# A gated WKV and feed-forward layer on one core: the recurrence in another form, a fixed slot for every step, and weight parts requested by ScalarE

## What is computed

```python
k = layernorm(x)                          # over the channels
# WKV recurrence over the 1024 tokens, for each of the 1024 channels, v = ctx
no = max(o, u + k_t); A = exp(o - no); E = exp(u + k_t - no)
y_t = (A*p + E*v_t) / (A*q + E)
no2 = max(w + o, k_t); A2 = exp(w + o - no2); E2 = exp(k_t - no2)
p, q, o = A2*p + E2*v_t, A2*q + E2, no2
x = x + tanh(g_xattn) * y
X = float16(layernorm(x))
D = float16(gelu(X @ W0.T + bias0))       # W0 is [4096, 1024]
x = x + tanh(g_ffn) * float16(D @ W1.T + bias1)   # W1 is [1024, 4096]
```

## Time and profile before

| | |
|---|---|
| median of 3 runs (range) | 2145.67 us (2144.49 to 2146.55) |
| span of the profiled execution | 2146.2 us |
| busy: PE, DVE, POOL, ACT | 1888.6, 1103.5, 592.7, 586.7 us |
| mean granted TensorE clock | 0.939 |
| moved by DMA | 286.56 MB, mean 134 GB/s |

### The profile page before, as it was taken

One profiled execution on the slowest core, in us unless ns is written; L12 is line 12 of the kernel. 1 busy time (PEld: TensorE's weight loads), 2 busy tenths in 40 slices (PEclk: granted clock), 3 DMA queues, 4 the chain that ended last, 5 costly groups with the idle time before them and its releaser, 6 DMA issues.

```text
span 2146.2 us, 23175 instructions
## 1 busy us (share of the span) xinstructions
PE 1888.6 (88%) x8960; PEld 892.4 (42%) x8960; DVE 1103.5 (51%) x1250; ACT 586.7 (27%) x759; POOL 592.7 (28%) x394
## 2 busy tenths in 40 slices
PE   1046778978889997999999997999999999999999
PEld 1023334434434443444444443444444444444444
DVE  8979975998971148899311158899211000000000
ACT  3326553343433232443000133443000121110000
POOL 4636750455653122444000022444000000000000
PEclk6558889989989998999999998999999999999999
DMA  5424574535466434333333333333233322223331
GB/s 176 142 103 156 168 254 169 212 119 205 164 229 197 156 117 139 108 126 126 122 118 118 138 128 118 127 127 140 90 115 118 108 79 79 79 88 112 108 110 53
DMA packets 72285, 286.56 MB, mean 134 GB/s; under 512 B 7680, under 2 KB 7680, under 8 KB 65024
## 3 DMA queue, kind: packets, MB, share of 16 engines
q1 hardware_dynamic: 72192, 285.28, 37.8%
HBM read 218.14 MB, written 67.11 MB: 133 GB/s over the span
## 4 chain that ended last, share of the span: by engine, by line
PE 68%; DVE 17%; issue 8%; POOL 3%; DMA 2%; ACT 1%; SPq 0%; DVEq 0%; POOLq 0%; ACTq 0%
PE acc L921 36%; PE acc L893 29%; DVE uOE L734 3%; DVE uOE L731 2%; DVE uOE L703 2%; DVE uA L712 1%; PE trA L856 1%; PE trA L872 1%; DVE uR L717 1%; DVE uOE L727 1%; DVE uR L722 1%; DVE K L745 1%; DVE uOE L709 1%; DVE uR L741 1%; DMA xin<-x_in 1%
## 5 line engine op out<-in xcount | busy, mean ns | idle before, releaser
L893 PE MATMUL acc<-XT,W 128*128 128x512 f16 x4096 | 911.7, 385 | 60.4 <-ACT DT L533 52.5
L921 PE MATMUL acc<-DT,W 128*128 128x512 f16 x4096 | 900.1, 381 | 12.1 <-POOL W L411 12.1
L893 PEld LDWEIGHTS acc<-XT,W 128*128 128x128 f16 x4096 | 405.8, 99 | 554.5 <-issue 66.7
L921 PEld LDWEIGHTS acc<-DT,W 128*128 128x128 f16 x4096 | 401.5, 98 | 491.1 <-issue 23.4
L757 DVE SCALAR_TENSOR_TENSOR xo<-e,tg,xo 128x512 f32<-128x512 f16 x64 | 52.1, 814 | 626.8 <-ACT e L542 626.6
L533 ACT ACTIVATE DT<-acc,b 128x512 f16<-128x512 f32 (+1 forms) x256 | 173.1, 686 | 511.2 <-PE acc L893 510.9
L542 ACT ACTIVATE e<-acc,b 128x512 f16<-128x512 f32 x64 | 43.8, 684 | 676.8 <-PE acc L921 676.8
L378 POOL TENSOR_TENSOR rstd<-rstd,power 128x1 f32<-128x1 f32 x64 | 47.5, 742 | 611.8 <-DVE rstd L646 611.8
L741 DVE RECIPROCAL uR<-uR 128x512 f32<-128x512 f32 x64 | 209.6, 3314 | 0.0
L391 POOL TENSOR_TENSOR uOE<-uOE,uV 128x512 f32<-128x512 f32 x64 | 81.0, 1275 | 380.4 <-ACT uOE L502 233.7
L640 DVE BATCH_NORM_STATS2 stats<-trA 128x6 f32<-128x512 f32 x60 | 38.8, 689 | 218.8 <-PE trA L872 218.8
(11 more groups left out here) (54 smaller groups left out, 1000.2 us busy)
## 6 DMA issues: line engine op xcount, KB each, us to landing
W<-parts_dram SPq DMA_DIRECT2D x56, 2048.0 KB, 8.1
parts_dram<-W SPq DMA_DIRECT2D x64, 512.0 KB, 6.7
stage<-w_in SPq DMA_DIRECT2D x52, 512.0 KB, 6.0
uV<-vT_in SPq DMA_DIRECT2D x64, 256.0 KB, 2.7
xT<-xT_in SPq DMA_DIRECT2D x32, 512.0 KB, 5.2
x_dram<-K SPq DMA_DIRECT2D x32, 512.0 KB, 3.7
xo<-x_dram SPq DMA_DIRECT2D x32, 512.0 KB, 9.6
out<-xo SPq DMA_DIRECT2D x32, 512.0 KB, 7.9
```

The source lines that it names most:

```text
L893: mm = nc.tensor.matmul(acc[bank][:, :], W[:, slot, part, q, P * c:P * (c + 1)], XT[:, c, HALF * half:HALF * (half + 1)], start=(c == 0 an ...
L921: mm = nc.tensor.matmul(acc[bank][:, :], W[:, slot, part, q, P * c:P * (c + 1)], DT[:, nb, HALF * half:HALF * (half + 1)], start=(nb == 0 ...
```

## The change

It does six things.

1. **The recurrence loses its running maximum.** With decay = exp(min(w, 0)), kept in `decay`, it scans `q` and `p` directly with E = exp(k + shift); a positive part of w is taken care of by adding `grow` times the token's number to the normalised rows (one more VectorE pass for each tile of `x`, 128x1024). A unit is now seven VectorE operations of 512 elements (E times V, scan q, scan p, denominator, numerator, reciprocal, product), three tiny copies, one exponential on ScalarE and one sum on GpSimd (`residual`).
2. **`K` is gone.** TensorE transposes four blocks into a pair of PSUM banks (`unit_banks`), the exponential is made there in place, and VectorE works on E and E·V in PSUM. `copy_k` is gone with it. Four PSUM banks serve the front, one the float16 transposes, so three are left as accumulators (`BANKS = 3`).
3. **One unit at a time at a fixed slot.** A batch has 128 slots of 16 matmuls. `UNIT_SLOT`, `LN1_SLOT` and `LN2_SLOT` say at which slot each unit, tile of `x` and tile of the second norm stands; every engine walks the same slots. The program is unrolled.
4. **The parts are requested by ScalarE** (`load_parts` in its program), except the first of each new pass in batch 0; the constants too, ahead of everything on ScalarE.
5. **`xin` holds four tiles**, and they are loaded after the last unit that reads the four before.
6. **SyncE's order** follows the slots: in a unit's slot it loads V for n + 2, waits until unit n has been summed (`x2_done`) and loads xT for n + 4.

The diff, cut to its core:

```diff
+SLOTS = 4 * NB
-BANKS = 4
+BANKS = 3
+RING1, RING2 = 5, 3
+def place_front():
+    for i, k in enumerate((5, 6, 9, 12, 14, 17, 20, 22)):
+        UNIT_SLOT[CB + i] = k
+    for i, k in enumerate((37, 38, 41, 44, 46, 49, 52, 54, 64, 65, 68, 71, 73, 76, 79, 81)):
+        UNIT_SLOT[UNITS + i] = k
+    for i in range(HT):
+        LN1_SLOT[HT + i] = 1 + i
+        LN1_SLOT[2 * HT + i] = 33 + i
+        LN1_SLOT[3 * HT + i] = 60 + i
+        LN2_SLOT[HT + i] = (27 + i, 29 + i)
+    for i in range(TILES):
+        LN2_SLOT[TILES + i] = (88 + 2 * i, 90 + 2 * i)
...
+    for b in (1, 2):
+        at, n, T = SLOTS * b, UNITS * (b + 1), TILES * (b + 1)
+        for i, k in enumerate((1, 4, 8, 12, 16, 20, 24, 28, 37, 40, 44, 48, 52, 56, 60, 64)):
+            UNIT_SLOT[n + i] = at + k
...
+        for i in range(TILES):
+            LN2_SLOT[T + i] = (at + 72 + 6 * i, at + 75 + 6 * i)
...
+        def parts_to_w(engine, s):
+            engine.dma_start(W[:, s % 2, :, :, :].rearrange("p a q n -> p (a q n)"), parts_dram[s])\
+                .then_inc(w_landed[s % 2], 16)
...
+            def load_xT(n):
+                b, i = divmod(n, UNITS)
+                if n >= 4:
+                    sp.wait_ge(x2_done, n - 3)
...
+            def residual(n):
+                pool.wait_ge(y_done, n + 1)
+                pool.wait_ge(xT_landed[n % 4], 16 * (n // 4 + 1))
+                slot = X2[:, n % UNITS, :]
+                nc.gpsimd.tensor_tensor(slot, slot, S[:, n % 2, 1, 0:HALF], ALU.add).then_inc(x2_done, 1)
...
+            def exps(n):
+                act.wait_ge(kt_done, n + 1)
...
+                bank = unit_banks(n)[0]
+                nc.scalar.activation(bank, bank, ACT.Exp, bias=shift[:, n % CB:n % CB + 1]).then_inc(e_ready, 1)
...
+            def load_parts(s, groups):
+                act.wait_ge(mm_done, groups)
+                parts_to_w(act, s)
...
+                    if b == 0 and NB <= k < 2 * NB - Q and k % Q == 0:
+                        load_parts((k - NB) // Q + 1, k)
+                    if b and k % (2 * Q) == 0 and not (b == B - 1 and k == SLOTS - 2 * Q):
+                        load_parts((k // (2 * Q) + 1) % (2 * STEPS),
+                                   GROUPS * b if k == 0 else group_of(b, k - 1) + 1)
+                    for n in UNITS_AT.get(K, ()):
+                        exps(n)
+                    if K in X2_AT:
+                        copy_xt(X2_AT[K])
+                    if k < GROUPS1:
+                        gelu(b, k)
+                    elif k % Q == Q - 1:
+                        round_e(b, (k - GROUPS1) // Q)
+                    if b == 0 and k < NB - 2 * Q:
+                        hi_piece(k + 2 * Q)
...
+            def norm_x(T):
+                row = xin[:, T % HT, :]
+                dve.wait_ge(rstd_done[0], T + 1)
+                nc.vector.tensor_scalar(row, row, mv[:, 0, T % 2, 0:1], rstd[:, 0, T % 2, 1:2],
+                                        ALU.subtract, ALU.mult).then_inc(xn_done, 1)
...
+                nc.vector.scalar_tensor_tensor(row, grow[:, :], negt[:, T % TILES:T % TILES + 1], row,
+                                               ALU.mult, ALU.add).then_inc(xn_ready, 1)
...
+            def unit(n):
...
+                nc.vector.tensor_copy(S[:, j, :, 0], state[:, i, :]).then_inc(seeded, 1)
+                dve.wait_ge(e_ready, n + 1)
+                nc.vector.tensor_tensor(EV, E, V[:, j, :], ALU.mult).then_inc(ev_done, 1)
+                dve.wait_ge(seeded, n + 1)
+                nc.vector.tensor_tensor_scan(S_q[:, 1:], decay[:, c:c + 1].to_broadcast([P, HALF]), E,
+                                             S_q[:, 0:1], ALU.mult, ALU.add).then_inc(q_done, 1)
+                dve.wait_ge(ev_done, n + 1)
+                nc.vector.tensor_tensor_scan(S_p[:, 1:], decay[:, c:c + 1].to_broadcast([P, HALF]), EV,
+                                             S_p[:, 0:1], ALU.mult, ALU.add).then_inc(p_done, 1)
+                dve.wait_ge(q_done, n + 1)
+                nc.vector.scalar_tensor_tensor(E, E, bonus[:, c:c + 1], S_q[:, 0:HALF], ALU.mult, ALU.add)\
+                    .then_inc(den_done, 1)
+                dve.wait_ge(p_done, n + 1)
+                nc.vector.scalar_tensor_tensor(EV, EV, bonus[:, c:c + 1], S_p[:, 0:HALF], ALU.mult, ALU.add)\
+                    .then_inc(num_done, 1)
...
+                nc.vector.reciprocal(S_q[:, 0:HALF], E).then_inc(rec_done, 1)
...
+                nc.vector.scalar_tensor_tensor(S_q[:, 0:HALF], EV, tg[:, 0:1], S_q[:, 0:HALF],
+                                               ALU.mult, ALU.mult).then_inc(y_done, 1)
...
+            dve.wait_ge(s_const, 16 * 7)
...
+            def unit(n):
...
+                pe.wait_ge(y_done, n - 1 if n >= CB else n - 2)
+                for j in range(HT):
+                    mm = transpose_piece(n, j)
+                mm.then_inc(kt_done, 1)
...
+            for b in range(B):
+                for k in range(SLOTS):
+                    K = SLOTS * b + k
+                    for n in UNITS_AT.get(K, ()):
+                        unit(n)
+                    if K in X2_AT:
+                        channels_x2(X2_AT[K])
+                    if K in X2T_AT:
+                        tokens_x2(X2T_AT[K])
...
+                    if k < GROUPS1:
+                        group1(b, k)
+                    else:
+                        quarter2(b, k)
```

More of the change, by code:

```diff
@@ L119, in build @@
         xo = sb("xo", [P, 2, L])
[L122 to L135, removed]
@@ L351, in _ @@
-            with sp.Fori(1, B - 1) as b:
-                first_product(b)
-                second_product(b, {0: 7})
-            first_product(B - 1, front=False)
-            second_product(B - 1, {}, front=False, more=False)
+            for T in range(HT):
+                load_x(T)
+            load_v(0)
+            load_v(1)
+            for n in range(4):
+                load_xT(n)
+            for g in range(RING1):
+                load_piece(g)
+            for n in range(CB):
+                load_v(n + 2)
+                if n < 4:
+                    for g in (2 * n, 2 * n + 1):
+                        store_piece(g)
+                        load_piece(g + RING1)
+                load_xT(n + 4)
+                if n % 2:
+                    store_x2(n)
+                if n == 5:
+                    for T in range(HT, 2 * HT):
+                        load_x(T)
@@ L1005, with quarter2 @@
-LEAD = 7
+            def quarter2(b, k):
+                g, q = divmod(k - GROUPS1, Q)
+                s, half = divmod(g, 2)
+                m = GROUPS * b + GROUPS1 + g
+                if b == 0 and half == 0:
+                    pe.wait_ge(lo_done, NB + Q * s + q + 1)
+                if b and half == 0 and q == 0:
+                    pe.wait_ge(w_landed[s % 2], 16 * (Q + CB * (b - 1) + Q + s // 2 + 1))
+                if q == 0:
+                    pe.wait_ge(acc_drained, m - BANKS + 1)
+                if g == 0 and q == Q - 1:
+                    pe.wait_ge(acc_drained, GROUPS * b + GROUPS1)
+                for c in range(CB):
+                    nb = CB * q + c
+                    for part in range(2):
+                        mm = nc.tensor.matmul(acc[m % BANKS][:, :], W[:, s % 2, part, q, P * c:P * (c + 1)],
+                                              DT[:, nb, HALF * half:HALF * (half + 1)],
+                                              start=(nb == 0 and part == 0), stop=(nb == NB - 1 and part == 1))
+                if q == Q - 1:
+                    mm.then_inc(mm_done, 1)
@@ new lines, in _ @@
+            pe.wait_ge(s_pool0, 6)
+            for j in range(HT):
+                pe.wait_ge(xn_ready, j + 1)
+                for n in range(3):
+                    mm = transpose_piece(n, j)
+                    if j == HT - 1:
+                        mm.then_inc(kt_done, 1)
+            for n in range(3, CB):
+                unit(n)
+            for T in range(HT):
+                tokens_x2(T)
+                if T:
+                    channels_x2(T - 1)
+            channels_x2(HT - 1)
@@ L1021 @@
         "x": np.asarray(x).reshape(B * TILES, P, H),
[L1023 removed]
+        "xT": units(x),
         "vT": units(ctx_2048),
```

1020 lines of the change are left out of this document (338 added, 682 removed).

## The result

The changed kernel takes 1995.45 us against 2145.67, a ratio of 0.9297 (95% interval 0.9283 to 0.9312). The forecast was 1964. The sign and most of the size came as forecast: 150 us gained, where 182 were worked out. 31 are missing.

The account below looks back on a forecast made before the run. TensorE's products, 442.0 us a batch, were taken as the floor, with start and stalls to win. 120 to the first group + 478.8 + 919.2 + 446.7 = 1964.7; forecast 1964, own range 1948 to 1985, stated range 1946 to 2000.

Parts of the forecast that it names:

- the 10 that were named: Sign in the first product: less than 10 us of waits for GELU, against 52.5 before.
- the requests are worth little: Requesting the 2 MB parts on ScalarE wins 7.5 us at most, TensorE's one wait for them before.
- That costs nothing: Batches 1 and 2: parts land in 8.1 us, due 27 after request, nothing queued behind; otherwise a late part costs 7.5.
- The argument from L651: Recurrence on VectorE: L651, tensor input in PSUM, stays at 1335 to 1345 ns, so no collision with GpSimd was counted.
- the rival of 1994: Recurrence's operations collide with GpSimd after all, a unit takes 11.7 us, the whole 1994; chance 0.12.
- a unit slow on PSUM: Scans and reciprocal slow on PSUM; 15.2 us a unit reaches 2146, 16 gives 2188; chance 0.02.
- the rate: Price per us of unit: 8 at the start above 8.9, 18 in batch 0's stretches above 9.5.
- table switches: ScalarE, batch 0's dense stretch: loads included in a 2 us stall; rival with costlier switches, 20 more, 1985, chance 0.03.
- the start: Up to the first product group: 120 us (112 to 130) against 151.2, with constants there at 9.5.
- I take 8.9, since GpSimd works about half of the time: VectorE's unit from start to start: 8.5 us, or 9.5 with copies held up by GpSimd; 8.9 taken.
- it stands until that unit is summed, some three slots: SyncE held in a unit's slot, pieces of weight queued behind: 2 us in batch 0, bounds 0 and 16.
- 470.8 + 8: Batch 0 from its first group: 470.8 us of TensorE's products, transposes and slow clock, plus 8 of stalls, 478.8.

Follow-up runs that it names:

- e5: Changed kernel with the next half's four tiles of x requested ahead of the load and store that wait for the unit's sum: 1978.72 us.
- e2: Changed kernel with the 2 MB parts requested by SyncE as before, no longer by ScalarE: 1994.26 us.
- e7: Changed kernel with a second reciprocal of 512 elements, into a scratch tile, in every unit: 2086.92 us.
- e9: e5 with the first product's GELU replaced by Identity, so ScalarE never switches tables (output not the layer's): 1974.43 us.
- e1: The changed kernel unaltered, profiled a second time: 1996.48 us; its profiled run of 1992.04 us supplies the rows of after.
- e4: Changed kernel with the copy seeding the next unit's scans (L519) moved behind the reciprocal, ahead of the unit's last product: 1987.83 us.
- e10: e6 with the copy that saves the state in the first eight units moved from VectorE to ScalarE: 1964.85 us.
- e6: Changed kernel with the edits of e3, e4 and e5 together: 1969.16 us.
- e8: Changed kernel without the pass that adds grow times token number to each tile of x (output not the layer's): 1972.0 us.
- e3: Changed kernel with the statistics of the first two tiles of x taken before VectorE waits for the constants: 1992.7 us.

## Why the prediction was right or wrong

**Right: what bounds the kernel, and where the gain comes from.** 1024 matmuls in 221 us, 459.6 for an undisturbed batch (459.58 in e5) and 446.7 for the last were exact. The waits for GELU fell from 52.5 to 2.6, below the 10 that were named.

**Right in size, and partly by luck: the requests are worth little.** At most 7.5 was said; e2 gives 2 us in the wrong direction, within its scatter. But it is a balance of 8.1 won in batch 0 and 6.8 lost in batches 1 and 2, where the prediction said "That costs nothing".

**Right: no collision of the recurrence's operations.** The argument from L651 carried over to scans, sums and reciprocals (the flat lines above), so the rival of 1994 falls, and that of a unit slow on PSUM too: a scan takes 1.18 from start to start, as counted, a reciprocal 3.35 against 3.31. That the total came out at 1995 proves nothing for the first of them; the operations that it named don't collide. Others do, which neither the sum nor the rival looked at: the copy L519 and, at slot 64, the two passes over x, of which the new one has two tensors in SBUF (`grow` and `xin`).

**Right: the rate.** 26 us per us of unit above 9.5 was the price in the rival of the slow unit; e7 paid (25.8 + 59.4) / 3.3 = 26. That it agrees so closely is luck, since only 35.6 of the 59.4 are the wait that was priced.

**Right: table switches.** 2 us of ScalarE's stall were counted, 20 more in a rival. e9 finds 2.5 in the dense stretch. The exponential begins right at the end of the table load, here as in the earlier trace rows (ScalarE of e1, batch 1):

```profile
699.28 0.33 ACTq L162 DMA_DIRECT2D W<-parts_dram  x1
...
699.98 1.28 ACT L379 ACT_TABLE_LOAD   x1
701.27 0.66 ACT L379 ACTIVATE front<-front,shift 128x512 f32<-128x512 f32 x1
701.95 1.28 ACT L414 ACT_TABLE_LOAD   x1
703.25 0.69 ACT L414 ACTIVATE DT<-acc,b 128x512 f16<-128x512 f32 x1
```

A switch takes 1.29 from the load's start to the activation's. The Trainium skill's drain of about 1380 ns (ScalarE: Activation LUTs, "What ACT_TABLE_LOAD costs") isn't there; its 1283 is. The first line also shows a request ahead of the unit that delays nobody.

**Wrong: the start, 127.7 for 120, by two terms.** The constants were taken at 9.5 and are there at 13.49 (VectorE's first instruction behind them; ScalarE's last two requests):

```profile
3.47 1.03 ACTq L365 DMA_DIRECT2D b<-bias_in  x2
...
13.49 0.17 DVE L553 TENSOR_SCALAR wp<-w_u 128x8 f32<-128x8 f32 x1 [13.49 <-DMA b<-bias_in]
```

The last request begins at 4.0, as the prediction let it, but takes 9.5 us to land and not the 3.85 of the earlier trace rows, with SyncE's loads under way. The seven land one behind another, the first (512 KB) 4.8 after its request and the six small ones 6.2, 7.1, 8.1, 9.0, 9.2 and 9.5. The last is there 4.0 later than the 9.5 that was taken. The small operations and the tiles were 1.4 shorter than counted. The eight units then took 5.3 more than 8 × 8.9, the copy L519 above all, and the rest 0.2 less: 4.0 − 1.4 + 5.3 − 0.2 = 7.7.

The failed sentence is "I take 8.9, since GpSimd works about half of the time". It took the copies' delay as a matter of chance, 0.6 at most from the median of 658 ns, and the delay was set by the code: the product just ahead of the copy releases GpSimd, and one copy held for 1.10 to 1.29 makes the 9.5 for which the prediction wanted two. In e4, which takes this copy out of the way, the first group came 5.3 sooner; in e10, which takes the other one away as well, 3.8 sooner than in e6. The Trainium skill bears on it (SBUF — State Buffer, "Who interferes with whom"; the same page says under "SBUF: two separate sides" that a float32 copy from SBUF to SBUF runs in a two-port mode): such a copy and a GpSimd operation shut each other out. The trace agrees, 1.10 beside a sum of 1.09 and 0.16 alone. The prediction had cited the rule for the unit's large operations and not asked it of the small ones, nor of the passes over x.

**Wrong: SyncE's order, and "That costs nothing" for batches 1 and 2.** The hold was seen ("it stands until that unit is summed, some three slots"), its bounds were 0 and 16 and 2 was taken. But it was priced for the pieces queued behind it, and they were not late: ScalarE waited 0.8 us for a piece in slots 5 to 22. What stands right behind the hold are the four tiles of x, once in each batch's front, with no slack: 12.8 of hold + 23.8 of way against 31.2. No step of the sum had this way from x's request to the next unit.

It cost batch 0 7.56 at slot 64, batch 1 8.2 with the low clock after it, batch 2 2.4. Taking the hold away (e5) gained 4.3 + 8.2 + 2.5 = 15.0 in the profiles, 17.8 in the medians; shortening the way at the other end did much the same (e8). Two more things lengthen the way, and e5 only makes room for them: the part that ScalarE requests beside the tiles, without which batch 1 loses 1.8 and not 8.2 (e2), and the 3.6 of collision at slot 64. This is the largest part of the miss. The prediction had most of the terms: loads of 512 KB, and 3.9 a tile for statistics, normalising and the new pass.

**Batch 0 besides.** In e5 it takes 481.8 against 470.8 + 8, and TensorE is idle in it for 8.5: 2.5 for GELU, 1.3 for XT at slot 32 and 0.9 for GpSimd's sum at slot 27 (predicted 2, 1.4 and 1.4), none behind a late piece (predicted 2), but 3.7 for x at slot 64, for which nothing was counted. Its busy time is 473.3 where 470.8 were counted.

**Open.** Why the constants land late beside SyncE's loads, and what decides whether the part holds up the second or the third tile of x. On the second question hangs, by the profiles of e1, e3 and e4, some 5.5 us in batch 2, as much as e1's five runs spread (5.3; e3's 7.9, against 1.8 for e5, where x comes early). That it makes the spread is likely and not shown: only one execution of each kernel has a profile.

## What to carry to other kernels

For every wait that a moved or reordered DMA queue contains, list each request behind it with its own due time, and add up hold, landing and the work up to its first user; the request that is made rarely and in a bunch is the one to examine, and what another engine requests at that moment is part of its landing. A small operation's median says little where its neighbour in the program is what releases the other engine: look at the two start times. And when a large wait is removed, the next one is found by asking what the stalled engine would have been late for anyway, as with parts and x in e2.

## What the hardware showed beyond that

A VectorE copy of two numbers a partition took 0.16 us or as long as GpSimd's instruction beside it, up to 2.1. Two passes of 128x1024 in SBUF took 5.65 beside GpSimd's pieces and 2.08 otherwise, while operations with a tensor in PSUM stayed flat. Four loads of 512 KB, requested together within 1.85 us with a load of 2 MB requested by ScalarE in between, had their first tile there after 5.2 and the second after 10.6; with the 2 MB behind them, the second after 6.9 at most. The granted clock is given as 0.99 for the 127 us ahead of the first group, in which TensorE is busy for 18.7; yet four transposes at 39.50 took 1.12 there, as they do at 0.50 (1.11 at 750.30), so the mean of such a stretch says little; before it was 0.58 with 19.7 of 151. In batch 1 an idle time of 5.3 us was followed by 31 matmuls at 295 ns, against 216 at full clock.
